# Cross attentions on one NeuronCore: outputs and softmax sums in separate products, q and k placed ahead of the maxima

## What is computed

```python
# xattn0: t = 256 positions (the channels), H = 8 heads of d = 8 (of the 64 tokens), band of 64
q, k, v = split(x @ w_in.T + b_in)
scores = einsum('bqhd,bkhd->bhqk', q, k) / sqrt(d)
scores = where(abs(i - j) <= 64, scores, -big)
o = einsum('bhqk,bkhd->bqhd', softmax(scores, axis=-1), v)
out = (relu(o @ w_out.T + b_out) * encodings) @ w_ct + b_ct
# xattn1: the same without band, projections and gate; q from x, k = v = the context
```

## Time and profile before

| | us |
|---|---|
| median of three runs | 2913.16 |
| profiled execution | 2907.95 |
| its span, first to last instruction | 2906.2 |
| xattn0 in it | about 457 to 1128 |
| clearing of the regions, no engine computing | about 1188 to 1208 |
| xattn1 in it | about 1870 to 2506 |
| mean granted clock of TensorE | 0.888 |

### The profile page before, as it was taken

One profiled execution on the slowest core, in us unless ns is written; L12 is line 12 of the kernel. 1 busy time (PEld: TensorE's weight loads), 2 busy tenths in 40 slices (PEclk: granted clock), 3 DMA queues, 4 the chain that ended last, 5 costly groups with the idle time before them and its releaser, 6 DMA issues. The chain is left out here.

```text
span 2906.2 us, 54662 instructions
## 1 busy us (share of the span) xinstructions
PE 2177.5 (75%) x18700; PEld 1525.1 (52%) x18700; DVE 1917.6 (66%) x5805; ACT 1170.6 (40%) x2616; POOL 899.7 (31%) x1488
## 2 busy tenths in 40 slices
PE   3554536888888883399998999388888888639986
PEld 2333324566566652399986777244444444416553
DVE  5999986676777777355555666477677767515345
ACT  1222213555555543122225666155555555313322
POOL 3444442222222222366660000222222222042622
PEclk8766667999999997699999999599999999769998
DMA  3000005443444340300000000544444444022444
GB/s 105 0 0 0 1 3 122 86 91 79 94 79 94 86 85 3 142 2 2 2 2 1 1 2 2 136 88 93 86 95 90 92 86 95 1 82 68 137 135 154
DMA packets 258066, 183.16 MB, mean 63 GB/s; under 512 B 34817, under 2 KB 252065, under 8 KB 257025
## 3 DMA queue, kind: packets, MB, share of 16 engines
q1 hardware_dynamic: 246176, 156.55, 23.8%
q0 software_dynamic: 7456, 18.92, 1.8%
q10 hardware_dynamic: 4160, 4.19, 0.5%
HBM read 94.47 MB, written 83.51 MB: 61 GB/s over the span
## 5 line engine op out<-in xcount | busy, mean ns | idle before, releaser
L750 ACT ACTIVATE xattn_pr<-ps 128x384 f32<-128x384 f32 (+1 forms) x1024 | 537.3, 543 | 449.0 <-PE ps L494 243.3
L478 PE MATMUL ps<-xattn_kp,xattn_qp 96*128 96x192 bf16 (+1 forms) x2048 | 383.1, 270 | 170.5 <-DMA xattn_kp<-xattn_rows 122.1
L624 DVE TENSOR_REDUCE xattn_mx<-ps 128x2 f32<-128x512 f32 x512 | 335.1, 677 | 186.8 <-PE ps L478 182.7
L491 PE MATMUL ps<-xattn_qp,xattn_kp 128*128 128x192 bf16 (+1 forms) x2048 | 419.8, 267 | 8.3 <-DMA xattn_qp<-xattn_mrow 7.7
L620 DVE CUSTOM_DVE_ANT_0 xattn_masked<-ps,xattn_band 128x192 bf16<-128x192 f32 x1024 | 325.3, 354 | 9.8 <-issue 6.3
L509 PE MATMUL ps<-xattn_pr,xattn_vs 128*32 128x256 f32 (+1 forms) x4096 | 313.6, 379 | 12.8 <-ACT xattn_o L755 12.6
L478 PEld LDWEIGHTS ps<-xattn_kp,xattn_qp 96*128 96x128 bf16 x2048 | 183.1, 101 | 237.6 <-DMA xattn_kp<-xattn_rows 115.9
L491 PEld LDWEIGHTS ps<-xattn_qp,xattn_kp 128*128 128x128 bf16 x2048 | 186.8, 99 | 144.4 <-ACT xattn_pr L750 79.4
L494 PE MATMUL ps<-xattn_band,xattn_ident 128*128 128x192 bf16 x1024 | 213.6, 249 | 0.0
L1973 PE MATMUL ps<-rwkv_xm,rwkv_w 128*128 128x256 f32 x384 | 122.0, 492 | 100.9 <-DVE rwkv_xm L2059 100.9
L981 PE MATMUL ps<-ffn_parts,gate_up_t 128*128 128x128 bf16 x3072 | 194.0, 220 | 2.1 <-DVE ffn_parts L1099 2.1
(11 more groups left out here) (305 smaller groups left out, 4460.2 us busy)
## 6 DMA issues: line engine op xcount, KB each, us to landing
xattn_rows<-xattn_parts SPq DMA_DIRECT2D x128, 192.0 KB, 2.1
xattn_qp<-xattn_rows SPq DMA_DIRECT2D x256, 96.0 KB, 3.3
xattn_kp<-xattn_rows SPq DMA_DIRECT2D x256, 96.0 KB, 3.7
xattn_rows<-xattn_parts SPq DMA_DIRECT2D x128, 128.0 KB, 2.1
moe_rows_in<-region_zero SPq DMA_DIRECT2D x6, 1677.0 KB, 7.3
moe_xb<-moe_rows_in SPq DMA_DIRECT2D x78, 129.0 KB, 2.2
xattn_rows<-xattn_parts SPq DMA_DIRECT2D x128, 64.0 KB, 1.8
moe_row<-moe_rows_out SPq DMA_DIRECT2D x16, 512.0 KB, 8.1
```

What stands on the lines that cost most here:

```text
L478: mm = nc.tensor.matmul(ps[:, BANK_S + j % RING, mt * D:mt * D + width], qp[u][s][0:R_MAX, h, mt * P:(mt + 1) * P], kp[u][s][0:R_MAX, h, l ...
L491: mm = nc.tensor.matmul(out, kp[u][s][:, h, nt * P:(nt + 1) * P], qp[u][s][:, h, lo:lo + width], start=True, stop=not banded)
L624: ins = nc.vector.tensor_reduce(mx[s][:, h * NT:(h + 1) * NT], ps[:, BANK_S + j % RING, :].rearrange("p (m n) -> p m n", m=NT), AX.X, ALU.max)
L750: nc.scalar.activation(out, src, ACT.Exp, scale=HD ** -0.5).then_inc(exped, 1)
```

## The change

1. **Separate products.** `vs` holds values only, in all four places of a quad, and a new tile `ones` holds ones. `multiply` has 16 parts for a pair where it had 8: outputs to one PSUM bank (`BANK_O`), sums to the next, in turn, one part in each slot from slot 3 on (the last three in the next step's slots 0 to 2). Outputs and sums come out in the order of `x`, so `align` and `C_SELECT` are gone. ACT's `keep_o` copies 256 columns twice, in slots 1 and 2, where it copied 512 once in slot 2. DVE reads SBUF (`o_sb`) and not PSUM, and its reciprocals stand in slots 3 and 4 and not 5 and 6; what follows moves by three slots, with PE's `gate_product` and `out_product`.
2. **Order of the placements.** SP's step places `(p + 2, 0)` ahead of the maxima of `(p + 1, 0)`, and that placement now waits, besides for the stores, for the transposed scores of the pair that used the buffer.
3. **Maxima in one DMA** to three rows of `qp`, where it was one DMA for each row.
4. **Clearing of the routed experts' regions** stands ahead of the causal attention, not of the feed-forward.

```diff
                 def place(p, u, s):
                     if s == 0:
                         sp.wait_ge(stored[u], by_parity(p, u, 96))
-                    else:
-                        wait(sp, scores_t, idx(p - 2, HW * (s + 1)))
+                    wait(sp, scores_t, idx(p - 2, HW * (s + 1)))
...
                 def place_maxima(p, u, s):
                     sp.wait_ge(max_kept, run(p, s) + 1)
-                    for part in range(PARTS):
-                        row = qp[u][s][R_MAX + part:R_MAX + part + 1, :, :].rearrange("a h (m n) -> a (h m) n", n=P)
-                        sp.dma_start(row, mrow[s][part * MX:(part + 1) * MX, :]).then_inc(rows_in[u][s], 16)
+                    rows = qp[u][s][R_MAX:R_MAX + PARTS, :, :].rearrange("r h (m n) -> r (h m) n", n=P)
+                    sp.dma_start(rows, mrow[s][:]).then_inc(rows_in[u][s], 16)
...
                     if there(p + 2):
                         store(p + 2, u)
+                        place(p + 2, u, 0)
                     if not last:
                         place_maxima(p + 1, 1 - u, 0)
                     if there(p + 2):
-                        place(p + 2, u, 0)
                         place(p + 2, u, 1)
...
                 def multiply(p, u, part):
-                    t, nt = divmod(part, NT)
-                    if nt == 0:
+                    t, (nt, sums) = part // QUAD, divmod(part % QUAD, 2)
+                    if part % QUAD == 0:
                         pe.wait_ge(exped, idx(p, QUAD * (t + 1)))
                     if part == 0:
                         pe.wait_ge(vo_ready, p + 1)
-                        wait(pe, o_kept, p)
-                    first = t % 2 == 0 and nt == 0
+                    if part < 2:
+                        wait(pe, o_kept, nth(p - 1, 2, part + 1))
+                    first = t == 0 and nt == 0
                     q = slice(0, D) if first or not banded else slice(nt * BAND, nt * BAND + WIN)
                     for g in range(QUAD):
-                        out = ps[g * COLS:(g + 1) * COLS, BANK_O, t // 2 * D + q.start:t // 2 * D + q.stop]
-                        mm = nc.tensor.matmul(out, vs[u][:, QUAD * g + t, nt, :], pr[(QUAD * t + g) % (2 * QUAD)][:, nt, q],
-                                              start=first, stop=(t % 2 == 1 and nt == NT - 1), tile_position=(0, g * COLS))
+                        w32 = ones[:, t, :] if sums else vs[u][:, QUAD * g + t, nt, :]
+                        mm = nc.tensor.matmul(ps[g * COLS:(g + 1) * COLS, BANK_O + sums, q], w32,
+                                              pr[(QUAD * t + g) % (2 * QUAD)][:, nt, q],
+                                              start=first, stop=(t == QUADS - 1 and nt == NT - 1), tile_position=(0, g * COLS))
                     mm.then_inc(multiplied, 1)
-                def align(p):
...
-                        if j % 2 == 1 and j > 1:
-                            multiply(p, u, (j - 3) // 2)
-                        elif j == 1 and not first:
-                            multiply(p - 1, 1 - u, TURNS - 1)
-                        if j == 4 and not first:
-                            align(p - 1)
+                        if j >= QUAD - 1:
+                            multiply(p, u, j - (QUAD - 1))
+                        elif not first:
+                            multiply(p - 1, 1 - u, NHS + j - (QUAD - 1))
...
                 def exponentials(p, j):
                     a.wait_ge(scores_t, idx(p, j) + 1)
-                    wait(a, multiplied, TURNS * p + 2 * (j // QUAD) - 2)
+                    wait(a, multiplied, idx(p, j // QUAD * QUAD) - QUAD)
...
-                        if j == 2 and not first:
-                            keep_o(p - 1)
+                        if j in (1, 2) and not first:
+                            keep_o(p - 1, j - 1)
```

More of the change, by code:

```diff
@@ L579, in step @@
                             project(p + 2, u)
-                        if banded and not first and j == 10:
+                        if banded and not first and j == 7:
                             gate_product(p - 1)
@@ L583, in step @@
                             make_values(p + 1, 1 - u)
-                        if banded and not first and j == 13:
+                        if banded and not first and j == 10:
                             out_product(p - 1)
@@ L812, in _ @@
                 over(a, PAIRS, step)
-                keep_o(PAIRS - 1)
+                for sums in range(2):
+                    keep_o(PAIRS - 1, sums)
             @block.gpsimd
```

86 lines of the change are left out of this document (35 added, 51 removed).

## The result

The changed kernel takes **2987.19 us** (median of 4 runs, 2981.78 to 2992.59) against 2912.62 us for the kernel before on the same chip: a ratio of 1.0256 with a 95% interval of 1.0237 to 1.0275. It is slower by 75 us. The forecast was 2997 us. The profiled execution took 2989.21 us, with a span of 2987.1 us.

The account below looks back on a forecast made before the run. Period bound: stores landed, hold-up, then 5.3 us placement. Late maxima add 30 x 1.3 + 30 x 1.4 = +81 us, stage ends +4, constants -1: 2907.95 + 84 = 2992 us profiled, 2997 us as median; range 2950 to 3065 us.

Parts of the forecast that it names:

- Direction and mechanism: Both wide attentions: slower, chance 0.85, because maxima issued behind the placement of q and k land late for TensorE's slot 14.
- The period: Length of one step per pair: +1.3 us in xattn0 to 21.1, +1.4 us in xattn1 to 20.2, before half a microsecond.
- stores landed: Time into a quiet step when SP's stores of rows are in memory: 13.0 us in xattn0, 12.2 us in xattn1.
- last of the four placements landed, from their start: Time from the start of placing q and k to the last landing: 5.3 us in xattn0, 5.2 us in xattn1.
- maxima landed behind it, and head 0 started: The merged maxima transfer lands 0.4 us after the last placement, letting head 0's transposed scores start; bounds 0.1 to 0.9 us.
- slots 14, 15 and the first product: TensorE's work between the maxima's landing and the next step, taken as 2.4 us in both stages.
- the added half microsecond: Excess of the mean period over 29 steps above the quiet steps read, 0.5 us, assumed to stay.
- three engines: Rival: merged maxima use three DMA engines, land 0.9 us behind the placement; +30 us, 3027 us, chance 0.25.
- The stores: Shift of the stores by the separate products ahead of them: +1.0 us in xattn1, -0.2 us in xattn0.
- TensorE itself: Rival: TensorE's path plus all parts, 20.4 us in xattn0, 19.9 in xattn1; without overlap 3067 us; chance 0.1.
- Two of the signs: Predicted trace evidence: changed TensorE waits, placement right after stores, maxima landing 3.3 to 4 then under 2 us, periods, stores' start.
- Clearing, constants and the ends of the stages: Outside the placing steps: moved clearing 0, smaller constants -1 us if anything, last steps of both stages +4 us.

## Why the prediction was right, point by point

**Direction and mechanism.** Right. The wait for k vanished, the wait for the maxima took its place, and its cause is that they stand behind the placement. Undoing the order alone gives 124 us back (2984 to 2860 us), and so, but for 9 us, does issuing the maxima elsewhere with the early placement kept.

**The period.** Forecast 21.6 and 20.7 us as means, found 21.64 and 20.74. The terms behind it, as means over 30 steps (us into a step):

| term | forecast | found |
|---|---|---|
| stores landed, xattn0 / xattn1 | 13.0 / 12.2 (quiet) | 13.85 / 12.82 |
| placement begins behind them | 0 | 0.02 |
| last of the four placements landed, from their start | 5.3 / 5.2 | 4.76 / 4.64 |
| maxima landed behind it, and head 0 started | 0.4 | 0.16 / 0.26 |
| slots 14, 15 and the first product | 2.4 | 2.86 / 3.0 |
| the added half microsecond | 0.5 | in the rows above |

The total came out closer than its terms, and that is luck: an overestimate of 0.8 and 0.7 us cancels what the other terms lack.

**The placement and the maxima behind it were taken too long.** The four placements landed 5.3 and 5.2 us after their start before, with three transfers of maxima just ahead of them, and land after 4.76 and 4.64 us now. The maxima land 2.85 and 2.92 us after their issue (means), 0.11 and 0.21 us behind the last placement, and in 9 of the 60 steps ahead of it, by up to 1.15 us. The step shown above is one of the nine: the last placement, issued at 700.82, lands 3.9 us later, at 704.7, and head 0 has started at 704.13.

```profile
xattn_kp<-xattn_rows SPq DMA_DIRECT2D x1, 96.0 KB, 3.9
```

So the price of "three engines", 0.9 us, and with it the rival's 3027 us, did not come. Its premise was not refuted. In the trace's semaphore records a transfer of one row gets 16 updates as it lands and the merged one gets four, in this step one at 702.56 and three from 703.90 to 704.09, which fits three engines; and with nothing ahead the merged transfer lands after 2.3 us, a row alone after 1.7 us. But its 48 packets all start within 0.4 us here (702.68 to 703.04), where my estimate had 0.85 us from the placements' pace. The rule on the number of engines that the prediction takes from the Trainium skill (DMA: Bandwidth & Descriptors) stands there in the section on why a DMA increments its semaphore by 16.

**The tail is longer**: 2.4 us is right at full clock (704.13 to 706.61 is 2.48 us), but in 10 and 11 of the 30 steps it runs in part at the lower clock and takes up to 3.9 and 4.4 us. As a mean 0.92 and 1.27 us of it are at the lower clock, and half of that is what it exceeds 2.4 us by.

**The half microsecond did not simply stay.** Before, the steps free of the lower clock took 20.15 and 19.00 us against means of 20.36 and 19.31, so by this comparison the clock made 0.2 and 0.3 us of it. It lay ahead of the stores and not in the tail: they landed 13.88 and 11.68 us into a step as a mean, against 13.2 and 11.2 in the two steps that I had read. The clock's share in the tail came on top.

**The stores.** The +1.0 us in xattn1 was +1.1 (11.68 to 12.82 us, means); the -0.2 us in xattn0 was 0.0. With the same order and the merged transfer but the old products the stores land 0.9 us later (14.79 us). They do so with the merged transfer alone as well (14.75 us), where TensorE waits for no maxima, so the wait for the maxima is not the reason; what is isn't shown.

**TensorE itself.** Forecast to be just hidden. The run without the order shows its own arrival: 15.7 us in xattn1, where I had 16.4, and a bare step of 18.2 us where the rival had 19.9. The rival took the wait for k out of the old path and left the others in it. Before, TensorE also waited 1.6 us a step in xattn1 for VectorE's maxima, ScalarE's copy and GpSimd's split; with the separate products these waits are gone, so that much of the 2.8 us of parts cost nothing.

**Two of the signs failed.** The maxima were to take 3.3 to 4 us to landing at the pair's start and under 2 us in its middle; they took 2.9 and 2.3 us. The others held: the waits, the placement 0.02 us behind the stores' landing, both periods, and the stores' start at 9.1 and 8.1 us.

**What I priced badly without harm to the total** is the merge. In the sum its saving on SP was worth nothing in the changed kernel. By itself it gains 73 us, and under the new order 32 us with the old products and 55 with the new. Of all four edits it is the one to keep.

**Clearing, constants and the ends of the stages.** 0, -1 and +4 us forecast. The clearing left in place makes 3 us between medians whose ranges overlap: nothing to tell. The other two were not tested alone; by the profiled executions the 30 steps make the whole difference, so together they are near 0.

## What to carry to other kernels

When one queue issues both a large transfer that is needed late and a small one that is needed early, let the small one go first and make it short to issue; here it cost the large one 0.3 to 0.4 us, since most of the issue fell where the large one couldn't start anyway. Before promoting a transfer, ask not only when its own consumer wants it, but what the one it overtakes holds up. And a wait that shrinks may not shorten the period by its length: here 1.1 us less of one wait brought 0.7 us more of two others.

## What the runs showed of the hardware

Waits of about 2 us in a stream of products that was otherwise full were followed by stretches of 3.4 us or more at a granted clock of 0.50. Such a stretch touched 14 and 17 of 30 steps with mean waits of 1.24 and 1.73 us, and all 30 with a mean wait of 2.49 us; without such waits the clock stayed at 1.00 for whole stages (596.76 us in the run without the order). The Trainium skill (TensorE: Matmul & The Clock Gate, the section What's actually happening) gives the same two levels, 1.2 and 2.4 GHz; the products drawn with 0.87 and 0.53 us in one step show the change between them.

A transfer of 48 pieces onto three rows of the destination landed 2.3 us after its issue with nothing ahead of it, and 2.9 us behind four queued placements of 192 pieces each. The Trainium skill (DMA: Bandwidth & Descriptors, on queues, rings and completion order) says that completion isn't in order of issue for one issuing engine. The trace agrees: in 9 of 60 steps of the changed kernel the maxima landed ahead of the last placement, which had been issued before them, by up to 1.15 us.
